# A Fourier mixing layer in fp32 on one core: the shared tile of the second layer as two matmuls of 64 rows, its bias written by VectorE

## The chip, the core and the metric

The kernel runs on one core of a Trainium2 chip. The metric is the device time of one execution in microseconds (us). Before the change it is 5919.63 us, the median of 3 runs (5910.64 to 5933.79).

## The reference

`x` has 4 images of 128 x 128 pixels and 768 channels. The channels are 8 blocks of 96, each with its own complex weights. What is computed, in fp32:

```
xf = rfft2(x, axes=(1, 2), norm='ortho')      # 128 x 65 frequencies
o1r = relu(xr @ w1[0] - xi @ w1[1] + b1[0]);  o1i = relu(xi @ w1[0] + xr @ w1[1] + b1[1])
o2r = o1r @ w2[0] - o1i @ w2[1] + b2[0];      o2i = o1i @ w2[0] + o1r @ w2[1] + b2[1]
o = softshrink(o2, 0.01)
out = irfft2(o, s=(128, 128), norm='ortho') + x
```

## The kernel before

One unit of work is one image and one block of 96 channels: 32 units, run in a loop of 16 pairs. A unit stays in on-chip memory from its load to its store. Its stages on TensorE are:

- A: the transform over the width, 128 matmuls of fp32 (L499). ScalarE copies the results to `U`.
- B, C, D: the rest of the forward transform and the two layers, in 33 steps of two frequencies each (step 32 has one frequency). B (L512, L513) is the first layer's product. C (L523) is the transform over the height. D (L538 to L544) is the second layer's product.
- flip (L549, L550): two matmuls that mend the two frequencies of step 0. ScalarE copies the result.
- E, F: the inverse transforms (L558, and L570 to L572), and VectorE adds the result to `x`.

The order is written out by hand on each engine, with semaphores between them. In the loop over s, TensorE issues B of step s, C of step s-1 and D of step s-2. ScalarE in the same turn copies B's result (L349), gathers the columns for step s+2 (L316), applies ReLU to C's result (L355, L358) and computes the first half of the soft shrinkage of D's result (`excess`, L367). VectorE computes ReLU once more and the low part (L440, L443), and then the shrinkage (L452).

The two frequencies of a step have 2 x 192 hidden values, real and imaginary part of 96 each. They lie in three tiles of 128 rows: the outer tiles 0 and 2 hold 128 values of one frequency each, and the shared middle tile 1 holds 64 values of either. In D an outer tile is multiplied in fp32 with 192 columns of its frequency's weights. The shared tile must add its upper 64 rows to one frequency's 192 columns and its lower 64 rows to the other's. Before, its activations and the weights are each split into a high and a low part of type fp32r (`hidden_high`, `hidden_low`, `w2_high`, `w2_low`, the weights padded with zeros), and three matmuls of 384 columns multiply them; a fourth, with `picks` and `b2_parts`, adds the bias of the second layer. On TensorE an fp32 matmul is two instructions, each with a weight load of its own; an fp32r matmul is one.

The banks of the accumulation memory (PSUM) in this stage: B 0 and 1, C's outer tiles 2 and 3, C's shared tile 6 and 7, D 4 and 5, each by the parity of the step. flip uses bank 6, E banks 4 to 6.

Of the kernel before, what the change touches and what calls it, by code (L numbers as in the profile page):

```python
# [88 lines left out]
def fourier_mlp(nc, x, w1, b1, w2, b2, dft, out):  # L89
    with ExitStack() as ctx:  # L90
# [18 lines left out]
        hidden = [sb(f"hidden{i}", [SIZE, 2, SIZE]) for i in range(2)]  # L109
        hidden_high, hidden_low = ([sb(f"hidden_{x}{i}", [SIZE, SIZE], F32R) for i in range(2)] for x in ("high", "low"))  # L110
        relu1 = [sb(f"relu1_{i}", [SIZE, SIZE]) for i in range(2)]

# [11 lines left out]

        w2_high, w2_low = (sb(f"w2_{x}", [SIZE, 4 * BLOCK], F32R) for x in ("high", "low"))
        over = sb("over", [SIZE, 1])
# [7 lines left out]
        b2_parts = sb("b2_parts", [SIZE, 2 * BLOCK], F32R)  # L134
        picks = sb("picks", [SIZE, SIZE], F32R)
        psum = ctx.enter_context(nc.psum_tensor("psum", [SIZE, 8, 512], F32))

        def bank(i, p=SIZE, n=512):
            return psum[0:p, i, 0:n]
# [15 lines left out]
        def bank_c(s):  # L155

            outer = bank(2 + s % 2, SIZE, 2 * SIZE)
            return [outer[:, 0:SIZE], bank(6 + s % 2, SIZE, SIZE), outer[:, SIZE:]]

        def bank_d(s):  # L160
            return bank(4 + s % 2, SIZE, 4 * BLOCK)

        def parts_d(s, rows):

            return bank_d(s).rearrange("p (q c) -> p c q", c=BLOCK)[:, :, 0:rows]

# [14 lines left out]
        w_loaded = [sem(f"w_loaded{i}") for i in range(2)]  # L181
        W_LOADS = 1 + 3 * len(SEGMENTS) + 2
# [3 lines left out]
        w_negated, w2_split = sem("w_negated"), sem("w2_split")  # L186
        high_done, relu1_done, low_done = sem("high_done"), sem("relu1_done"), sem("low_done")
        u_zeroed = sem("u_zeroed")
# [4 lines left out]
        d_done, excess_done, shrunk = sem("d_done"), sem("excess_done"), sem("shrunk")  # L193
        b2_split = sem("b2_split")
        flip_done, flip_copied = sem("flip_done"), sem("flip_copied")
# [27 lines left out]
        def _(sp):  # L223
# [83 lines left out]
        def _(act):  # L307
# [12 lines left out]
            with act.Fori(0, PAIRS) as m:  # L320
                for par in range(2):
# [22 lines left out]
                    for s in range(NS + 2):  # L344
# [34 lines left out]
        def _(dve):  # L379
            for t in (w2_high, w2_low):  # L380
                dve.memset(t[HALF:SIZE, 0:2 * BLOCK].bitcast(F32), 0.0).then_inc(padding_set, 1)
                dve.memset(t[0:HALF, 2 * BLOCK:].bitcast(F32), 0.0).then_inc(padding_set, 1)
# [3 lines left out]
            dve.wait_ge(padding_set, 7)  # L386
            for row in (0, LOW_ROW):
# [20 lines left out]
            with dve.Fori(0, PAIRS) as m:  # L408
                for par in range(2):
# [11 lines left out]

                    dve.wait_ge(w_negated, (n + 1) * (1 + len(NEGATED)))
                    halves = [(slice(0, HALF), slice(0, 2 * BLOCK)), (slice(HALF, SIZE), slice(2 * BLOCK, 4 * BLOCK))]
                    for rows, cols in halves:
                        dve.tensor_copy(w2_high[rows, cols], w2t[par][rows, 2 * BLOCK:4 * BLOCK]).then_inc(w2_split, 1)
                    dve.tensor_copy(b2_parts[0:1, :], b2t[par][0:1, :]).then_inc(b2_split, 1)
# [3 lines left out]
                                      ALU.subtract).then_inc(b2_split, 1)  # L430
                    dve.wait_ge(w2_split, n * 4 + 2)
                    for rows, cols in halves:
                        dve.tensor_tensor(w2_low[rows, cols], w2t[par][rows, 2 * BLOCK:4 * BLOCK], w2_high[rows, cols],
                                          ALU.subtract).then_inc(w2_split, 1)
                    for s in range(NS + 1):
                        if s < NS:

                            dve.wait_ge(high_done, n * NS + (s + 1))
                            dve.tensor_scalar(relu1[s % 2][:, :], bank_c(s)[1], b1t[par][:, 1:2], 0.0,  # L440
                                              ALU.add, ALU.max).then_inc(relu1_done, 1)
                            dve.wait_ge(relu1_done, n * NS + (s + 1))
                            dve.tensor_tensor(hidden_low[s % 2][:, :], relu1[s % 2][:, :], hidden_high[s % 2][:, :],  # L443
                                              ALU.subtract).then_inc(low_done, 1)
                        if s > 0:
# [37 lines left out]
        def _(pe):  # L483
# [43 lines left out]
            def stage_d(par, n, s):  # L527
                if s == 0:
                    pe.wait_ge(w2_split, n * 4 + 4)
                    pe.wait_ge(b2_split, n * 3 + 3)  # L530
                pe.wait_ge(relu_done, n * NS + (s + 1))
                pe.wait_ge(low_done, n * NS + (s + 1))
                if s >= 2:
                    pe.wait_ge(shrunk, n * NS + (s - 1))
                one, both = 2 * BLOCK, len(STEPS[s]) * 2 * BLOCK
                h, high, low, w, sums_d = hidden[s % 2], hidden_high[s % 2], hidden_low[s % 2], w2t[par], bank_d(s)
                bias = b2_parts[:, :].unsqueeze(1).broadcast_to([SIZE, len(STEPS[s]), 2 * BLOCK])
# [37 lines left out]
            pe.wait_ge(mats_loaded, 16)  # L575
            pe.wait_ge(padding_set, 9)
            with pe.Fori(0, PAIRS) as m:
# [37 lines left out]
```

## Time and profile before

| | |
|---|---|
| median of 3 runs | 5919.63 us |
| profiled execution, its own time | 5931.3 us |
| its span | 5929.5 us |
| granted TensorE clock, mean | 0.986 of full speed |
| TensorE matmuls busy | 97% of the span |
| ScalarE, VectorE, GpSimd busy | 62%, 52%, 21% |

The span is the time of the profiled program from its first to its last instruction. "Busy" of an engine is the time in which at least one of its instructions is under way. PE is TensorE, PEld its weight loads, ACT ScalarE, DVE VectorE, POOL GpSimd. A matmul's recorded duration holds the time until its result is out, and matmuls overlap, so the pace is read from the distance between starts.

### The profile page before, as it was taken

What the parts mean: (1) busy time and instruction counts of PE and PEld (TensorE: products, weight loads), DVE (VectorE), ACT (ScalarE), POOL (GpSimd) and SP (SyncE); (2) the same over time, 40 slices, a digit from 0 to 9 for tenths busy, and PEclk for the clock granted to TensorE, in tenths of its full rate; (3) what the DMA queues carried; (4) which work ended last, traced back from release to release, by engine and by line L of the source; (5) the groups of instructions that cost most, each with busy time, mean ns of one, the idle gap of its engine ahead of it and who ended that gap; (6) DMA issues with size and microseconds to landing.
All of it is one profiled execution on the core that took longest, in us unless ns stands there. A gap on an engine that the chain in (4) does not pass through costs nothing.

```text
span 5929.5 us, 116828 instructions
## 1 busy us (share of the span) xinstructions
PE 5750.8 (97%) x42048; PEld 5699.5 (96%) x42048; DVE 3077.5 (52%) x6166; ACT 3655.1 (62%) x8208; POOL 1263.1 (21%) x810
## 2 busy tenths in 40 slices
PE   8999999999999999999999999999999999999997
PEld 8999999999999999999999999999999999999997
DVE  4555545555455554555545555455554455544555
ACT  6656666566665666656566565665656656566564
POOL 2211222202222022220222202222022221122200
PEclk9999999999999999999999999999999999999999
DMA  3331133321333113332133321333312333123311
GB/s 94 89 89 40 50 89 89 89 50 41 89 89 89 46 44 89 89 89 59 33 88 89 89 68 31 80 89 89 79 34 66 89 89 87 39 53 89 89 44 43
DMA packets 1109645, 423.36 MB, mean 71 GB/s; under 512 B 1108768, under 2 KB 1108896, under 8 KB 1109024
## 3 DMA queue, kind: packets, MB, share of 16 engines
q1 hardware_dynamic: 1109024, 415.14, 27.8%
q8 instruction: 382, 6.26, 0.4%
q14 instruction: 239, 1.96, 0.1%
HBM read 213.75 MB, written 201.33 MB: 70 GB/s over the span
## 4 chain that ended last, share of the span: by engine, by line
PE 96%; issue 2%; ACT 1%; DVE 1%; DMA 0%; DVEq 0%; SPq 0%; ACTq 0%
PE psum L499 16%; PE psum L523 12%; PE psum L512 12%; PE psum L558 12%; PE psum L513 12%; PE psum L542 6%; PE psum L544 6%; PE psum L538 3%; PE psum L570 3%; PE psum L541 3%; PE psum L540 3%; PE psum L539 3%; PE psum L571 3%; PE psum L572 3%; DVE x L465 1%
## 5 line engine op out<-in xcount | busy, mean ns | idle before, releaser
L440 DVE TENSOR_SCALAR relu<-psum,b1t 128x128 f32<-128x128 f32 x1056 | 370.3, 351 | 1936.2 <-ACT hidden_high L355 1936.1
L289 POOL TENSOR_TENSOR doubled<-x 128x768 f32<-128x768 f32 x248 | 359.0, 1447 | 4337.2 <-DMA x<-x 4317.0
L512 PE MATMUL psum<-w1t,columns 96*128 96x192 f32 x4160 | 1035.8, 331 | 66.7 <-ACT columns L313 66.7
L513 PE MATMUL psum<-w1t,columns 96*128 96x192 f32 x4160 | 1029.7, 329 | 0.0
L499 PEld LDWEIGHTS psum<-mats,x 128*96 128x96 f32 x8192 | 930.0, 168 | 76.4 <-issue 54.2
L499 PE MATMUL psum<-mats,x 128*96 128x128 f32 x8192 | 939.1, 278 | 65.5 <-issue 48.8
L349 ACT ACTIVATE mixed<-psum 128x384 f32<-128x384 f32 (+1 forms) x1056 | 513.6, 486 | 746.7 <-PE psum L513 741.6
L376 ACT ACTIVATE sums_high<-psum 128x512 fp32r<-128x512 f32 x768 | 460.0, 599 | 763.7 <-PE psum L558 763.7
L523 PE MATMUL psum<-mats,mixed 128*128 128x128 f32 x6272 | 877.3, 276 | 0.0
L523 PEld LDWEIGHTS psum<-mats,mixed 128*128 128x128 f32 x6272 | 845.5, 193 | 0.0
L512 PEld LDWEIGHTS psum<-w1t,columns 96*128 96x128 f32 x4160 | 756.1, 199 | 73.5 <-ACT columns L313 73.5
L452 DVE SCALAR_TENSOR_TENSOR spectrum<-psum,excess 128x384 f32<-128x384 f32 (+1 forms) x1024 | 562.7, 549 | 491.3 <-ACT excess L367 489.4
L558 PE MATMUL psum<-mats,spectrum 128*128 128x128 f32 x6144 | 799.7, 275 | 11.4 <-ACT spectrum L370 11.4
L367 ACT ACTIVATE excess<-psum,over 128x384 f32<-128x384 f32 (+1 forms) x1056 | 608.8, 576 | 262.4 <-PE psum L544 245.7
L558 PEld LDWEIGHTS psum<-mats,spectrum 128*128 128x128 f32 x6144 | 742.7, 191 | 21.3 <-issue 21.3
L513 PEld LDWEIGHTS psum<-w1t,columns 96*128 96x128 f32 x4160 | 755.0, 198 | 0.0
L458 DVE TENSOR_TENSOR sums_low<-psum,sums_high 128x512 fp32r<-128x512 f32 x768 | 531.3, 692 | 307.5 <-ACT sums_high L376 307.5
L316 ACT ACTIVATE columns<-spectrum 96x512 f32<-96x512 f32 (+1 forms) x1024 | 686.5, 670 | 0.0
L358 ACT ACTIVATE hidden<-psum,b1t 128x128 f32<-128x128 f32 x2080 | 640.1, 361 | 0.0
L443 DVE TENSOR_TENSOR hidden_low<-relu,hidden_high 128x128 fp32r<-128x128 f32 x1056 | 566.0, 536 | 36.3
L465 DVE SCALAR_TENSOR_TENSOR x<-x,psum 128x260 f32<-128x260 f32 (+1 forms) x1536 | 564.6, 413 | 0.0
L542 PE MATMUL psum<-w2t,hidden 128*128 128x192 f32 x2112 | 515.5, 326 | 0.0
(61 smaller groups left out, 8437.8 us busy)
## 6 DMA issues: line engine op xcount, KB each, us to landing
x<-x SPq DMA_DIRECT2D x160, 768.0 KB, 7.2
out<-x SPq DMA_DIRECT2D x160, 768.0 KB, 8.2
x<-x SPq DMA_DIRECT2D x32, 1488.0 KB, 9.7
out<-x SPq DMA_DIRECT2D x32, 1488.0 KB, 10.6
x<-x SPq DMA_DIRECT2D x32, 816.0 KB, 5.0
out<-x SPq DMA_DIRECT2D x32, 816.0 KB, 4.5
w2t<-L_conv_w SPq DMA_DIRECT2D x128, 36.0 KB
w2t<-L_conv_w SPq DMA_DIRECT2D x128, 24.0 KB
```

What stands on the lines that cost most here:

```text
L316: last = act.activation(dst[:, 0:k], U[0:BLOCK, :, j:j + 2 * k].rearrange("p s (k r) -> p k s r", r=2), ACT.Copy)
L358: last = act.activation(hidden[t % 2][:, tile // 2], bank_c(t)[tile], ACT.Relu, bias=b1t[par][:, tile:tile + 1])
L367: act.activation(excess[t % 2][:, :, 0:rows], parts_d(t, rows), ACT.Relu, bias=over[:, 0:1]).then_inc(excess_done, 1)
L443: dve.tensor_tensor(hidden_low[s % 2][:, :], relu1[s % 2][:, :], hidden_high[s % 2][:, :], ALU.subtract).then_inc(low_done, 1)
L452: dve.scalar_tensor_tensor(dst, parts_d(t, rows), LAMBDA, excess[t % 2][:, :, 0:rows], op0=ALU.add, op1=ALU.min).then_inc(shrunk, 1)
L465: dve.scalar_tensor_tensor(part, part, 0.5, bank_f(q - LAG, j), op0=ALU.mult, op1=ALU.add).then_inc(f_added, 1)
L499: last = pe.matmul(bank_a(at)[:, i * SIZE:(i + 1) * SIZE], xs[par][:, slot, :], mat(FW_EVEN if slot <= HALF else FW_ODD), start=True, stop ...
L512: pe.matmul(bank_b(s)[:, k], re, w1t[par][:, BLOCK:], start=True, stop=False)
L513: last = pe.matmul(bank_b(s)[:, k], im, w1t[par][:, :2 * BLOCK], start=False, stop=True)
L523: last = pe.matmul(bank_c(s)[tile], flat[:, tile * SIZE:(tile + 1) * SIZE], mat(FH), start=True, stop=True)
L542: last = pe.matmul(sums_d[:, 0:one], h[:, 0], w[:, 0:one], start=False, stop=both == one)
L558: last = pe.matmul(bank_e(q)[:, :, i], U[:, q * CHUNK + i, 2:], mat(IH), start=True, stop=True)
```

## The change

The shared tile's activations are kept once, in fp32 (`middle`, by VectorE). D multiplies rows 0 to 63 of it with rows 0 to 63 of the weights for the first frequency, and rows 64 to 127 for the second, as fp32 matmuls that use 64 rows of the array each. Each frequency has a PSUM bank of its own, so D takes two banks for each parity of the step (4 and 5, 6 and 7), and C has banks 2 and 3 for all steps. From step 2 on, no matmul adds the bias: VectorE writes it into D's banks (`seeded`) two steps ahead, and all of D's matmuls add to it. In steps 0 and 1 the bias matmul stays, once for each frequency. C of a step now waits for the readers of the step before instead of the one before that, and flip waits for the shrinkage of step 31, since bank 6 is D's now.

```diff
-            return [outer[:, 0:SIZE], bank(6 + s % 2, SIZE, SIZE), outer[:, SIZE:]]
+            outer = bank(2, SIZE, 2 * SIZE)
+            return [outer[:, 0:SIZE], bank(3, SIZE, SIZE), outer[:, SIZE:]]
         def bank_d(s):
-            return bank(4 + s % 2, SIZE, 4 * BLOCK)
+            pair = psum[:, 4 + 2 * (s % 2):6 + 2 * (s % 2), :].rearrange("p k n -> p (k n)")
+            return pair.rearrange("p (q n) -> p q n", q=4)[:, :, 0:BLOCK]
@@ SyncE, load_w @@
+                put(b2_rows[par][:, :, :], b2[:, blk].partition_broadcast(SIZE))
@@ ScalarE, each step @@
-                            act.activation(hidden_high[t % 2][:, :], bank_c(t)[1], ACT.Relu,
-                                           bias=b1t[par][:, 1:2]).then_inc(high_done, 1)
@@ VectorE, once a unit @@
-                        dve.tensor_copy(w2_high[rows, cols], w2t[par][rows, 2 * BLOCK:4 * BLOCK]).then_inc(w2_split, 1)
-                        dve.tensor_tensor(w2_low[rows, cols], w2t[par][rows, 2 * BLOCK:4 * BLOCK], w2_high[rows, cols],
-                                          ALU.subtract).then_inc(w2_split, 1)
@@ VectorE, each step @@
-                            dve.wait_ge(high_done, n * NS + (s + 1))
-                            dve.tensor_scalar(relu1[s % 2][:, :], bank_c(s)[1], b1t[par][:, 1:2], 0.0,
-                                              ALU.add, ALU.max).then_inc(relu1_done, 1)
-                            dve.wait_ge(relu1_done, n * NS + (s + 1))
-                            dve.tensor_tensor(hidden_low[s % 2][:, :], relu1[s % 2][:, :], hidden_high[s % 2][:, :],
-                                              ALU.subtract).then_inc(low_done, 1)
+                            dve.wait_ge(c_done, n * NS + (s + 1))
+                            dve.tensor_scalar(middle[s % 2][:, :], bank_c(s)[1], b1t[par][:, 1:2], 0.0,
+                                              ALU.add, ALU.max).then_inc(middle_done, 1)
 ...
+                            if s + 1 < NS:
+                                k = len(STEPS[s + 1])
+                                dve.wait_ge(shrunk, n * NS + s)
+                                dve.tensor_copy(bank_d(s + 1).rearrange("p (k r) c -> p k r c", r=2)[:, 0:k],
+                                                b2_rows[par][:, :, :].unsqueeze(1).broadcast_to([SIZE, k, 2, BLOCK])).then_inc(seeded, 1)
@@ TensorE, stage_c @@
-                if s >= 2:
-                    pe.wait_ge(relu_done, n * NS + (s - 1))
-                    pe.wait_ge(relu1_done, n * NS + (s - 1))
+                if s >= 1:
+                    pe.wait_ge(relu_done, n * NS + s)
+                    pe.wait_ge(middle_done, n * NS + s)
@@ TensorE, stage_d @@
-                pe.matmul(sums_d[:, 0:both].rearrange("p (k o) -> p k o", o=2 * BLOCK), picks[:, :], bias, start=True, stop=False)
-                pe.matmul(sums_d[:, 0:both], high[:, :], w2_high[:, 0:both], start=False, stop=False)
-                pe.matmul(sums_d[:, 0:both], low[:, :], w2_high[:, 0:both], start=False, stop=False)
-                pe.matmul(sums_d[:, 0:both], high[:, :], w2_low[:, 0:both], start=False, stop=False)
-                last = pe.matmul(sums_d[:, 0:one], h[:, 0], w[:, 0:one], start=False, stop=both == one)
-                if both > one:
-                    last = pe.matmul(sums_d[:, one:both], h[:, 1], w[:, 2 * one:], start=False, stop=True)
+                for k in kws if s < 2 else ():
+                    pe.matmul(sums_d[k], picks[:, :], b2_parts[:, :].rearrange("p (r c) -> p r c", r=2), start=True, stop=False)
+                for k in kws:
+                    pe.matmul(sums_d[k], h[:, k], outer[k].rearrange("p (r c) -> p r c", r=2), start=False, stop=False, skip_group_check=s >= 2)
+                for k in kws:
+                    half = slice(k * HALF, (k + 1) * HALF)
+                    last = pe.matmul(sums_d[k], mid[half, :], w[half, 2 * BLOCK:4 * BLOCK].rearrange("p (r c) -> p r c", r=2),
+                                     start=False, stop=True, skip_group_check=s >= 2)
@@ TensorE, flip @@
-                pe.wait_ge(shrunk, n * NS + 1)
+                pe.wait_ge(shrunk, n * NS + (NS - 1))
```

TensorE's queue in a step of the middle of a unit, before: C of one step, D of the step before it, then the wait ahead of the next B. Names are those of the tiles; each fp32 row is two instructions on the chip.

```order
L523 MATMUL psum<-mats,mixed 128x128 [waits relu1_done,relu_done,b_copied]
L523 MATMUL psum<-mats,mixed 128x128 x2
L538 MATMUL psum<-b_parts,picks 128x384 [waits shrunk,low_done,relu_done]
L539 MATMUL psum<-w_high,hidden_high 128x384
L540 MATMUL psum<-w_high,hidden_low 128x384
L541 MATMUL psum<-w_low,hidden_high 128x384
L542 MATMUL psum<-w2t,hidden 128x192
L544 MATMUL psum<-w2t,hidden 128x192
L509 REGISTER_ALU [waits b_copied]
```

The same place now:

```order
L517 MATMUL psum<-mats,mixed 128x128 [waits middle_done,relu_done,b_copied]
L517 MATMUL psum<-mats,mixed 128x128 x2
L527 REGISTER_ALU [waits middle_done,relu_done]
L534 MATMUL psum<-w2t,hidden 128x2x96 [waits seeded]
L534 MATMUL psum<-w2t,hidden 128x2x96
L538 MATMUL psum<-w2t,middle 128x2x96 x2
L503 REGISTER_ALU [waits b_copied]
```

The four fp32r matmuls ahead of the outer tiles are gone, and the two matmuls of 64 rows stand behind them, last ahead of the next B. D's waits for `low_done` and `shrunk` are now waits for `middle_done` and `seeded`.

VectorE's queue in two steps of the middle of a unit, before:

```order
L439 REGISTER_ALU
L440 TENSOR_SCALAR relu_0<-psum,b1t 128x128 [waits high_done]
L443 TENSOR_TENSOR hidden_low<-relu_0,hidden_high 128x128 [waits relu1_done]
L452 SCALAR_TENSOR_TENSOR spectrum<-psum,excess 128x96x4 [waits excess_done]
L439 REGISTER_ALU
L440 TENSOR_SCALAR relu_1<-psum,b1t 128x128 [waits high_done]
```

And now:

```order
L431 REGISTER_ALU
L432 TENSOR_SCALAR middle<-psum,b1t 128x128 [waits c_done]
L441 SCALAR_TENSOR_TENSOR spectrum<-psum,excess 128x96x4 [waits excess_done]
L446 COPY psum<-b_rows 128x4x96 [waits shrunk]
L431 REGISTER_ALU
L432 TENSOR_SCALAR middle<-psum,b1t 128x128 [waits c_done]
```

The subtraction ahead of the shrinkage is gone, and a copy into PSUM stands behind it, ahead of the next `middle`.

## Rows read from the trace of the kernel before

**Rows 1.** The page's parts 1 and 2: busy time, and the granted clock.

```profile
PE 5750.8 (97%) x42048; PEld 5699.5 (96%) x42048; DVE 3077.5 (52%) x6166; ACT 3655.1 (62%) x8208; POOL 1263.1 (21%) x810
...
PEclk9999999999999999999999999999999999999999
```

**Rows 2.** The chain that ended last, by engine.

```profile
PE 96%; issue 2%; ACT 1%; DVE 1%; DMA 0%; DVEq 0%; SPq 0%; ACTq 0%
```

**Rows 3.** Busy time in one step: stretch, its length, each engine, clock, DMA.

```profile
2499.80:2503.13 3.33, 3.33 (x25) 3.33 (x24) 1.20 (x3) 2.41 (x6) 0.00 (x0) 1.00 0.02 5
```

**Rows 4.** Timeline of TensorE in that step: start, duration, instruction.

```profile
2500.49 0.33 PE L539 MATMUL psum<-w_high,hidden_high 128*128 128x384 f32 x1
...
2500.66 0.34 PE L540 MATMUL psum<-w_high,hidden_low 128*128 128x384 f32 x1
...
2500.83 0.35 PE L541 MATMUL psum<-w_low,hidden_high 128*128 128x384 f32 x1
...
2501.02 0.49 PE L542 MATMUL psum<-w2t,hidden 128*128 128x192 f32 x2
...
2501.34 0.49 PE L544 MATMUL psum<-w2t,hidden 128*128 128x192 f32 x2
...
2501.67 0.49 PE L512 MATMUL psum<-w1t,columns 96*128 96x192 f32 x2
2501.84 0.35 PEld L513 LDWEIGHTS psum<-w1t,columns 96*128 96x128 f32 x2
...
2501.99 0.49 PE L513 MATMUL psum<-w1t,columns 96*128 96x192 f32 x2
...
2502.64 0.49 PE L513 MATMUL psum<-w1t,columns 96*128 96x192 f32 x2
...
2502.97 0.83 PE L523 MATMUL psum<-mats,mixed 128*128 128x128 f32 x6
```

**Rows 5.** Groups by line: ScalarE and VectorE in the steps; busy, mean ns.

```profile
L316 ACT ACTIVATE columns<-spectrum 96x512 f32<-96x512 f32 x992 | 672.7, 678 | 0.0
...
L358 ACT ACTIVATE hidden<-psum,b1t 128x128 f32<-128x128 f32 x2080 | 640.1, 361 | 0.0
...
L367 ACT ACTIVATE excess<-psum,over 128x384 f32<-128x384 f32 x1024 | 595.0, 581 | 245.7 <-PE psum L544 245.7
...
L452 DVE SCALAR_TENSOR_TENSOR spectrum<-psum,excess 128x384 f32<-128x384 f32 x992 | 551.2, 556 | 478.7 <-ACT excess L367 476.8
...
L349 ACT ACTIVATE mixed<-psum 128x384 f32<-128x384 f32 x1024 | 503.0, 491 | 744.5 <-PE psum L513 741.6
...
L440 DVE TENSOR_SCALAR relu<-psum,b1t 128x128 f32<-128x128 f32 x1056 | 370.3, 351 | 1936.2 <-ACT hidden_high L355 1936.1
```

**Rows 6.** Timeline around D of steps 31 and 32 and flip, all engines.

```profile
2542.41 0.49 PE L544 MATMUL psum<-w2t,hidden 128*128 128x192 f32 x2
...
2542.60 0.29 DVE L443 TENSOR_TENSOR hidden_low<-relu,hidden_high 128x128 fp32r<-128x128 f32 x1
...
2542.93 0.58 ACT L367 ACTIVATE excess<-psum,over 128x384 f32<-128x384 f32 x1 [0.70 <-PE psum L544]
...
2542.96 0.19 PEld L538 LDWEIGHTS psum<-b_parts,picks 128*128 128x128 f32 x1 [0.36 <-issue]
...
2543.07 0.19 PEld L539 LDWEIGHTS psum<-w_high,hidden_high 128*128 128x128 f32 x1
...
2543.27 0.27 PE L540 MATMUL psum<-w_high,hidden_low 128*128 128x192 f32 x1
...
2543.38 0.27 PE L541 MATMUL psum<-w_low,hidden_high 128*128 128x192 f32 x1
...
2543.55 0.56 DVE L452 SCALAR_TENSOR_TENSOR spectrum<-psum,excess 128x384 f32<-128x384 f32 x1 [0.66 <-ACT excess L367]
...
2543.84 0.84 PE L549 MATMUL psum<-real_kw,mats 128*128 128x192 f32 x2
```

More of the change, by code:

```diff
@@ L109, in fourier_mlp @@
         hidden = [sb(f"hidden{i}", [SIZE, 2, SIZE]) for i in range(2)]
-        hidden_high, hidden_low = ([sb(f"hidden_{x}{i}", [SIZE, SIZE], F32R) for i in range(2)] for x in ("high", "low"))
-        relu1 = [sb(f"relu1_{i}", [SIZE, SIZE]) for i in range(2)]
+        middle = [sb(f"middle{i}", [SIZE, SIZE]) for i in range(2)]
         excess = [sb(f"excess{i}", [SIZE, BLOCK, 4]) for i in range(2)]
@@ L123, in fourier_mlp @@
         w2t = [sb(f"w2t{i}", [SIZE, 6 * BLOCK]) for i in range(2)]
-        w2_high, w2_low = (sb(f"w2_{x}", [SIZE, 4 * BLOCK], F32R) for x in ("high", "low"))
         over = sb("over", [SIZE, 1])
@@ L135, in fourier_mlp @@
         picks = sb("picks", [SIZE, SIZE], F32R)
+        b2_rows = [sb(f"b2_rows{i}", [SIZE, 2, BLOCK]) for i in range(2)]
         psum = ctx.enter_context(nc.psum_tensor("psum", [SIZE, 8, 512], F32))
@@ L155, in bank_c @@
         def bank_c(s):
-            outer = bank(2 + s % 2, SIZE, 2 * SIZE)
-            return [outer[:, 0:SIZE], bank(6 + s % 2, SIZE, SIZE), outer[:, SIZE:]]
+            outer = bank(2, SIZE, 2 * SIZE)
+            return [outer[:, 0:SIZE], bank(3, SIZE, SIZE), outer[:, SIZE:]]
         def bank_d(s):
-            return bank(4 + s % 2, SIZE, 4 * BLOCK)
+            pair = psum[:, 4 + 2 * (s % 2):6 + 2 * (s % 2), :].rearrange("p k n -> p (k n)")
+            return pair.rearrange("p (q n) -> p q n", q=4)[:, :, 0:BLOCK]
         def parts_d(s, rows):
-            return bank_d(s).rearrange("p (q c) -> p c q", c=BLOCK)[:, :, 0:rows]
+            return bank_d(s).rearrange("p q c -> p c q")[:, :, 0:rows]
         bank_flip = bank(6, SIZE, 2 * BLOCK).rearrange("p (k c) -> p k c", k=2)
@@ L181, in fourier_mlp @@
         w_loaded = [sem(f"w_loaded{i}") for i in range(2)]
-        W_LOADS = 1 + 3 * len(SEGMENTS) + 2
+        W_LOADS = 1 + 3 * len(SEGMENTS) + 3
         mats_loaded, iw_loaded = sem("mats_loaded"), sem("iw_loaded")
@@ L185, in fourier_mlp @@
         padding_set = sem("padding_set")
-        w_negated, w2_split = sem("w_negated"), sem("w2_split")
-        high_done, relu1_done, low_done = sem("high_done"), sem("relu1_done"), sem("low_done")
+        w_negated = sem("w_negated")
+        middle_done = sem("middle_done")
         u_zeroed = sem("u_zeroed")
@@ L193, in fourier_mlp @@
         d_done, excess_done, shrunk = sem("d_done"), sem("excess_done"), sem("shrunk")
-        b2_split = sem("b2_split")
+        b2_split, seeded = sem("b2_split"), sem("seeded")
         flip_done, flip_copied = sem("flip_done"), sem("flip_copied")
@@ L379, in _ @@
         def _(dve):
-            for t in (w2_high, w2_low):
-                dve.memset(t[HALF:SIZE, 0:2 * BLOCK].bitcast(F32), 0.0).then_inc(padding_set, 1)
-                dve.memset(t[0:HALF, 2 * BLOCK:].bitcast(F32), 0.0).then_inc(padding_set, 1)
             dve.memset(over[:, :], -LAMBDA).then_inc(padding_set, 1)
@@ L385, in _ @@
             dve.memset(picks[:, :].bitcast(F32), 0.0).then_inc(padding_set, 1)
-            dve.wait_ge(padding_set, 7)
+            dve.wait_ge(padding_set, 3)
             for row in (0, LOW_ROW):
@@ L420, in _ @@
                         dve.tensor_scalar(part, part, -1.0, None, ALU.mult).then_inc(w_negated, 1)
-                    dve.wait_ge(w_negated, (n + 1) * (1 + len(NEGATED)))
-                    halves = [(slice(0, HALF), slice(0, 2 * BLOCK)), (slice(HALF, SIZE), slice(2 * BLOCK, 4 * BLOCK))]
-                    for rows, cols in halves:
-                        dve.tensor_copy(w2_high[rows, cols], w2t[par][rows, 2 * BLOCK:4 * BLOCK]).then_inc(w2_split, 1)
                     dve.tensor_copy(b2_parts[0:1, :], b2t[par][0:1, :]).then_inc(b2_split, 1)
@@ L430, in _ @@
                                       ALU.subtract).then_inc(b2_split, 1)
-                    dve.wait_ge(w2_split, n * 4 + 2)
-                    for rows, cols in halves:
-                        dve.tensor_tensor(w2_low[rows, cols], w2t[par][rows, 2 * BLOCK:4 * BLOCK], w2_high[rows, cols],
-                                          ALU.subtract).then_inc(w2_split, 1)
                     for s in range(NS + 1):
                         if s < NS:
-                            dve.wait_ge(high_done, n * NS + (s + 1))
-                            dve.tensor_scalar(relu1[s % 2][:, :], bank_c(s)[1], b1t[par][:, 1:2], 0.0,
-                                              ALU.add, ALU.max).then_inc(relu1_done, 1)
-                            dve.wait_ge(relu1_done, n * NS + (s + 1))
-                            dve.tensor_tensor(hidden_low[s % 2][:, :], relu1[s % 2][:, :], hidden_high[s % 2][:, :],
-                                              ALU.subtract).then_inc(low_done, 1)
+                            dve.wait_ge(c_done, n * NS + (s + 1))
+                            dve.tensor_scalar(middle[s % 2][:, :], bank_c(s)[1], b1t[par][:, 1:2], 0.0,
+                                              ALU.add, ALU.max).then_inc(middle_done, 1)
                         if s > 0:
@@ L528, in stage_d @@
                 if s == 0:
-                    pe.wait_ge(w2_split, n * 4 + 4)
                     pe.wait_ge(b2_split, n * 3 + 3)
                 pe.wait_ge(relu_done, n * NS + (s + 1))
-                pe.wait_ge(low_done, n * NS + (s + 1))
+                pe.wait_ge(middle_done, n * NS + (s + 1))
                 if s >= 2:
-                    pe.wait_ge(shrunk, n * NS + (s - 1))
-                one, both = 2 * BLOCK, len(STEPS[s]) * 2 * BLOCK
-                h, high, low, w, sums_d = hidden[s % 2], hidden_high[s % 2], hidden_low[s % 2], w2t[par], bank_d(s)
@@ L542, in stage_d @@
-                last = pe.matmul(sums_d[:, 0:one], h[:, 0], w[:, 0:one], start=False, stop=both == one)
-                if both > one:
-                    last = pe.matmul(sums_d[:, one:both], h[:, 1], w[:, 2 * one:], start=False, stop=True)
+                    pe.wait_ge(seeded, n * (NS - 2) + (s - 1))
+                h, mid, w, kws = hidden[s % 2], middle[s % 2], w2t[par], range(len(STEPS[s]))
+                sums_d = [bank_d(s)[:, 2 * k:2 * k + 2] for k in kws]
+                outer = [w[:, 0:2 * BLOCK], w[:, 4 * BLOCK:]]
@@ L575, in _ @@
             pe.wait_ge(mats_loaded, 16)
-            pe.wait_ge(padding_set, 9)
+            pe.wait_ge(padding_set, 5)
             with pe.Fori(0, PAIRS) as m:
```

1 line of the change is left out of this document (removed).

## The prediction, made before the changed kernel ran

> **What bounds the kernel now.** I read the page's busy line first, then the chain of waits, then one step in detail. TensorE's matmuls are busy 97% of the span at a granted clock of 0.9 or more of full speed in every slice [rows 1], the upper of the two levels (2.4 GHz), and the chain that ended last runs over TensorE for 96% [rows 2]. No other engine is above 62%. So a change counts by what it adds to or takes from TensorE's queue, and by the waits that reach it.
>
> The stage that changes is a repeated step of 3.33 us, in which TensorE is busy 3.33 us, ScalarE 2.41 us and VectorE 1.20 us [rows 3]. A unit has 33 steps, the kernel 1056. Before that, 30 steps of each unit (2 to 31) are alike: 960 in all; steps 0 and 1 (64) and step 32 (32) are counted apart.
>
> In a step the pace is the distance between starts [rows 4]. An fp32 product of 192 columns (two instructions) takes 2501.34 - 2501.02 = 0.32 to 0.33 us, so 0.1625 us for each instruction; Recorded durations are longer: a pair shows 0.49 us where it holds the queue for 0.325, so a result is out 0.165 us behind the queue's time. C's six instructions show 0.83, less 0.165 that is 0.67, or 0.11 each. An fp32r matmul of 384 columns comes each 0.17 us. The weight load of the next instruction begins when the present matmul begins (load at 2501.84, its matmul at 2501.99), and is hidden.
>
> **What goes from a step.** The four fp32r matmuls. The step is 3.33; B is four products and D's outer tiles two, six times 0.325 = 1.95; C is 6 x 0.11 = 0.67. What is left is 3.33 - 1.95 - 0.67 = 0.71 us, which is 4 x 0.17 and 0.03 us for going from fp32 to fp32r and back. This 0.71 us stands wholly on the path.
>
> **What comes to a step: two fp32 products of 64 rows and 192 columns.** That is four instructions, and no row of before shows a matmul of 64 rows; B's 96 rows run at the pace of 128 (0.325 for a product, rows 4), so fewer rows alone save nothing. What can save is that the lower and the upper half of the array work at once. Bounds:
> - No overlap: 4 x 0.1625 = 0.65 us.
> - Full overlap: 2 x 0.1625 = 0.325 us.
 Weight loads come at 0.11 us at the closest [rows 6]: there two loads start at 2542.96 and 2543.07, and the fp32r matmuls of 192 columns, whose columns would take half of 0.17, start 0.11 apart, at 2543.27 and 2543.38. With the loads in order, the third instruction starts at 2 x 0.11 = 0.22, the fourth at 0.22 + 0.1625 = 0.38, and the pair is through at 0.54 us.
> I take 0.54 us: it is the value between the bounds that the order of the queue and the spacing of the loads give.
>
> The TensorE page of the Trainium skill (TensorE: Matmul & The Clock Gate, Part 3, packing small matmuls) says that matmuls on different row groups start about 4 ns apart, in program order. No row here shows it. By that alone the third instruction would start with the second, at 0.16, and the pair would take 0.49.
>
> **Switching the array between 128 and 64 rows, twice a step.** The trace of before has no such switch. The lower bound is nothing. The upper is a full stop: the array empties (the 0.165 us by which a result is late) and the next weights are loaded in the open (0.11 us, the load spacing behind the idle time in rows 6), 0.275 us a switch, 0.55 a step. The nearest row is the switch from fp32 to fp32r and back, 0.03 us for both; I take twice that, 0.06 us a step.
>
> Here a page speaks against the change. The Trainium skill (TensorEngine Tiling (Array Packing), Key Properties) says that changing the tiling mode, not just the tile, drains TensorE, without a price. By the cheap switch of the rows the step gets shorter, by a full drain longer; this is the third rival below.
>
> So a middle step changes by -0.71 + 0.54 + 0.06 = -0.11 us, times 960 = -106 us.
>
> **Steps 0 and 1** keep a bias matmul, one for each frequency: two of 192 columns at 0.11 and the type switch 0.03, +0.25. Together -0.71 + 0.25 + 0.60 = +0.14 us, times 64 = +9 us.
>
> **Step 32 and flip.** Before, flip starts at 2543.84; D of step 31 left the queue at 2542.41 + 0.325 = 2542.74, so 1.10 us earlier [rows 6]. Now flip waits for the shrinkage of step 31: `excess` starts 0.19 us behind the queue's end (2542.93), takes 0.58, and the shrinkage starts 0.04 later (2543.55) and takes 0.56; with 0.03 for the semaphore 0.19 + 0.58 + 0.04 + 0.56 + 0.03 = 1.40, say 1.43. D of step 32, 0.65 us of matmuls, hides in that, with the wait for `middle`, for which VectorE must first seed step 32. Before, TensorE waited here too (0.36 us without a load, for `hidden_low`). So +0.33 us a unit, times 32 = +10 us. Behind flip are ScalarE's copy and E, as before.
>
> **What costs nothing, and its cover.** ScalarE loses one ReLU of the step and has 0.49 + 0.68 + 2 x 0.36 + 0.58 = 2.47 us of work [rows 5] in a step of about 3.2. VectorE has 0.35 (middle) + 0.56 (shrinkage) and the seed. The seed is a copy of 384 elements from on-chip memory into PSUM, which no row shows; bounds 0.35 (the row of 128 elements) and 0.56 (the row of 384 elements); I take 0.5. That is 1.4 us of 3.2. The seed stands ahead of `middle` in the queue: D out at 0.17, `excess` to about 0.8, shrinkage to 1.4, seed to 1.9, and C's result comes at 1.30 + 0.67 + 0.17 = 2.1 us, so `middle` isn't late. The new wait of C is for ReLU of the step before. ScalarE does it behind the copy of B (1.5 to 2.0) and the gather (to 2.7), so to 3.4 us; the next C is due at 3.2 + 1.3 = 4.5 us, 1.1 us later. B's gather, behind C's wait in no queue of another engine, keeps its place. The seed of a step is needed a whole step later. The added load of the bias rows (128 partitions) is issued a unit ahead. All of this is cover that stays if the step falls to about 2.9 us; at full overlap (2.95 us) it is still just there.
>
> **The sum.** -106 + 9 + 10 = -87 us against the profiled execution's own 5931.3, so 5844; that execution lies 0.2% above the median of the runs, so 5832 us against 5919.63 (-1.5%).
>
> **The rivals.**
> 1. Full overlap of the two halves. It needs the hardware to run both pairs side by side though they stand behind one another. The 128 rows of the array speak for it, the order of the queue against it. Step -0.71 + 0.325 + 0.06 = -0.325, times 960 = -312, steps 0 and 1 at -0.075 = -5, flip +10: -307 us, 5613 us.
> 2. The change doesn't do what it says: the halves run one behind the other. Step -0.71 + 0.65 + 0.06 = 0; steps 0 and 1 at +0.25 = +16, flip +10: +26 us, 5946 us, just about no change. For it: both pairs are fp32 pairs with loads of their own, and 96 rows show no gain. Against: different banks and different rows leave nothing shared but the queue.
> 3. Slower: the array stops at each switch of its rows, in D ahead of the 64-row matmuls and again ahead of the next B. With the load alone in the open, 2 x 0.11 = 0.22: step +0.05 = +48, steps 0 and 1 at +0.30 = +19, flip +10: +77, 5997 us. With a full stop, 0.55: step +0.38 = +365, steps 0 and 1 at +0.63 = +40, +10: +415, 6335 us. It decides from 0.17 us of switching a step, 0.085 a switch, less than one load in the open; with halves that don't overlap, from 0.06. For it: between different uses of the array each load must be timed anew, and no slack is left on an engine that is busy without a gap. Against: the switch of type costs 0.03.
> 4. VectorE or ScalarE becomes the bound: 2.47 and 1.4 us in 3.2 speak against it, and I leave it inside the range.
>
> **How the numbers follow.** Forecast 0.40 (its own range 5760 to 5900), full overlap 0.08, no overlap 0.15, stops at the switch 0.37, about evenly spread between its two prices. A measurement of this kernel tells a change from none at about 0.5%, 30 us. Faster: 0.38 of the forecast and 0.08 = 0.46. The same: 0.02 and 0.10 of "no overlap" = 0.12. Slower: 0.05 and 0.37 = 0.42. The range leaves out about a tenth on either side: 5640 to 6300.
>
> **What the profile would show.** Distance between the starts of C in the middle of a unit: 3.22 us for the forecast, 3.0 for full overlap, 3.33 for none, 3.38 to 3.71 for stops. The start of the second 64-row product behind the first: 0.22 for the forecast, 0.325 for no overlap, next to nothing for full. A stop shows as a start of B, or of the first 64-row matmul, more than 0.2 us behind the one before it, with its load later than that one's start. VectorE's copy into PSUM between 0.35 and 0.56 us. Flip 1.4 us behind the queue's end of D of step 31. The forecast is wrong if a switch costs over 0.08 us, or if C or D wait for ScalarE or VectorE in the middle steps.

## The result, and the profile after

| | before | after |
|---|---|---|
| median | 5919.63 us (5910.64 to 5933.79, 5 runs) | 5960.43 us (5954.12 to 5967.26, 5 runs) |
| ratio | | 1.0066, 95% interval 1.0049 to 1.0083 |
| span of the profiled execution | 5929.5 us | 5958.6 us |
| granted TensorE clock in it, mean | 0.986 | 0.990 |
| one step in the middle of a unit | 3.33 us | 3.35 us |

The kernel is slower by 0.7%. The forecast was 1.5% faster. Two terms of the sum failed, in opposite directions: the two halves overlap wholly (0.215 us a step better than forecast), and each change between 128 and 64 rows of the array costs 0.20 us (0.34 us a step worse).

The page's busy line of the changed kernel, the answer to [rows 1]:

```profile
PE 5777.4 (97%) x42112; PEld 5259.3 (88%) x42112; DVE 3033.5 (51%) x5970; ACT 3379.7 (57%) x7152; POOL 1251.2 (21%) x810
...
PEclk9999999999999999999999999999999999999999
```

TensorE is still the bound. In the middle of a unit it had its full clock in both kernels (1.00); over the whole execution the mean rose from 0.986 to 0.990, which is taken up below. What is new stands in PEld: the weight loads were busy as long as the matmuls (96%) and are now at 88%. Loads that wait are the mark of the change. Where they wait is in the list of waits (line waited on, releaser: total us, times, longest):

```profile
PEld psum L538 <- issue: 237.6, 1056, 0.2
PEld psum L506 <- issue: 215.9, 960, 0.2
...
PEld psum L534 <- DVE psum L446: 18.3, 32, 0.7
...
PE psum L534 <- DVE middle L432: 9.0, 32, 0.4
...
PEld psum L544 <- DVE spectrum L441: 7.2, 32, 0.2
```

In every one of 1056 steps the load of the first 64-row matmul (L538) finds its queue idle for 0.23 us, with nothing of another engine that releases it, and in 960 steps so does the load of the next B (L506). Before, no such row stands in the middle steps of a unit. The same in the timeline of one step (start, duration, instruction), which answers to [rows 4]:

```profile
2501.50 0.83 PE L517 MATMUL psum<-mats,mixed 128*128 128x128 f32 x6
...
2502.17 0.82 PE L534 MATMUL psum<-w2t,hidden 128*128 128x192 f32 x4
...
2502.91 0.30 PEld L538 LDWEIGHTS psum<-w2t,middle 64*128 64x128 f32 x4 [0.23 <-issue]
2502.92 0.60 PE L538 MATMUL psum<-w2t,middle 64*128 64x192 f32 x4
2503.44 0.31 PEld L506 LDWEIGHTS psum<-w1t,columns 96*128 96x128 f32 x2 [0.23 <-issue]
2503.44 0.60 PE L506 MATMUL psum<-w1t,columns 96*128 96x192 f32 x2
...
2503.88 0.49 PE L507 MATMUL psum<-w1t,columns 96*128 96x192 f32 x2
```

Read it as a sum of distances. The outer tiles start at 2502.17 and hold the queue for 4 x 0.1625 = 0.65, to 2502.82. The load of the 64-row matmul starts only at 2502.91, 0.09 later, together with its matmul; in [rows 4] a load starts a whole matmul ahead. The four 64-row instructions then take 2503.44 - 2502.92 = 0.52 us. B's first product takes 2503.88 - 2503.44 = 0.44 where it took 0.325 before, 0.11 of it the load in the open. If the same 0.09 and 0.11 stand around the 64-row matmuls, 0.52 - 0.20 = 0.32 us is left for all four: that is the price of two, so the halves run side by side. In all 0.325 + 2 x 0.20 = 0.73 us, against the 0.71 us of the four fp32r matmuls. A narrower window, up to 2502.99, shows two starts at 2502.92, so two instructions begin together:

```profile
2502.92 0.43 PE L538 MATMUL psum<-w2t,middle 64*128 64x192 f32 x2
```

Here x2 covers 0.43 us; a single one of them lasts up to 0.427 (0.11 more than the 0.32 of one whose load is hidden). The other two begin together as well, at 2503.18 and 2503.19. A row doesn't say which half an instruction belongs to, and ends of matmuls are modelled, so this reading needed experiments.

Where the 29.1 us of span went, added up over the 32 units from the starts in the traces: from the first to the last start in C 3321.3 before and 3355.5 us after, +34; from there to flip 82.3 and 88.7, +6; from a unit's first start in B to its first in C 111.9 and 94.9, -17; everything else +6. The -17 is TensorE's clock and not a saving of the change. That stretch takes 5.28 us at the lower of the two levels and 2.71 at the upper, here in two units of the kernel before (stretch, its length, each engine, clock, DMA):

```profile
2621.67:2626.95 5.28, 5.28 (x16) 5.28 (x17) 0.00 (x0) 1.58 (x3) 2.82 (x2) 0.50 1.17 325
3172.06:3174.77 2.71, 2.71 (x16) 2.71 (x17) 0.00 (x0) 1.58 (x3) 0.00 (x0) 1.00 0.26 60
```

Before, 15 of the 32 units take longer than 2.71 us there; after, 6. Over the whole execution TensorE stood at the lower level for 41 us less than before, apart from the end, where it is idle. That is worth about 20 us (an estimate: at half the clock half of the time is lost), so at an equal clock the changed kernel would be nearer 50 us slower than 29. The runs show the same bond of time and clock: on one chip the kernel before took 5950 to 5952 us at a granted clock of 0.983 and 5912 to 5915 at 0.989; the one run of the changed kernel at 0.989 took 5967. TensorE's wait ahead of the stretch is the same in both (66.7 us in 32 waits for `columns`); why the changed kernel falls to the lower level less often, no run here shows.

### The profile page after: what moved, and what is told of

Its sections match the earlier page's. It is cut to its first block, busy times and chain, and to the rows that moved or that the text cites. A ratio compares the mean times of both kernels' runs of the same rounds, so it can differ in the third digit from the quotient of the medians.

```text
span 5958.6 us, 116726 instructions
## 1 busy us (share of the span) xinstructions
PE 5777.4 (97%) x42112; PEld 5259.3 (88%) x42112; DVE 3033.5 (51%) x5970; ACT 3379.7 (57%) x7152; POOL 1251.2 (21%) x810
## 4 chain that ended last, share of the span: by engine, by line
PE 95%; issue 2%; ACT 1%; DVE 1%; DMA 0%; DVEq 0%; SPq 0%; ACTq 0%
PE psum L493 15%; PE psum L506 15%; PE psum L553 12%; PE psum L517 12%; PE psum L507 11%; PE psum L534 11%; PE psum L538 9%; PE psum L565 3%; PE psum L566 3%; PE psum L567 3%; DVE x L459 1%; PE psum L544 0%; ACT columns L319 0%; PE psum L545 0%; ACT excess L371 0%
## 5 line engine op out<-in xcount | busy, mean ns | idle before, releaser
L506 PE MATMUL psum<-w1t,columns 96*128 96x192 f32 x4160 | 1132.4, 354 | 66.7 <-ACT columns L319 66.7
L507 PE MATMUL psum<-w1t,columns 96*128 96x192 f32 x4160 | 1021.2, 327 | 0.0
L493 PE MATMUL psum<-mats,x 128*96 128x128 f32 x8192 | 933.5, 277 | 64.3 <-issue 47.3
L506 PEld LDWEIGHTS psum<-w1t,columns 96*128 96x128 f32 x4160 | 701.3, 196 | 289.4 <-issue 215.9
L432 DVE TENSOR_SCALAR middle<-psum,b1t 128x128 f32<-128x128 f32 x1056 | 370.0, 350 | 1015.7 <-PE psum L517 1015.7
L534 PE MATMUL psum<-w2t,hidden 128*128 128x192 f32 x4160 | 855.6, 328 | 9.0 <-DVE middle L432 9.0
L507 PEld LDWEIGHTS psum<-w1t,columns 96*128 96x128 f32 x4160 | 750.4, 197 | 0.0
L534 PEld LDWEIGHTS psum<-w2t,hidden 128*128 128x128 f32 x4160 | 652.9, 191 | 18.3 <-DVE psum L446 18.3
L538 PE MATMUL psum<-w2t,middle 64*128 64x192 f32 x4160 | 629.0, 375 | 0.0
```

What stands on the lines that cost most here:

```text
L493: last = pe.matmul(bank_a(at)[:, i * SIZE:(i + 1) * SIZE], xs[par][:, slot, :], mat(FW_EVEN if slot <= HALF else FW_ODD), start=True, stop ...
L506: pe.matmul(bank_b(s)[:, k], re, w1t[par][:, BLOCK:], start=True, stop=False)
L507: last = pe.matmul(bank_b(s)[:, k], im, w1t[par][:, :2 * BLOCK], start=False, stop=True)
L534: pe.matmul(sums_d[k], h[:, k], outer[k].rearrange("p (r c) -> p r c", r=2), start=False, stop=False, skip_group_check=s >= 2)
L538: last = pe.matmul(sums_d[k], mid[half, :], w[half, 2 * BLOCK:4 * BLOCK].rearrange("p (r c) -> p r c", r=2), start=False, stop=True, skip_ ...
```

## The experiments

Two theories. "Stops": the halves overlap wholly and a change of rows costs 0.20 us. "No overlap": the halves follow one another (0.65 us) and changes are nearly free (0.04 each). Both give the measured 0.73 us a step. Each ratio below is to the kernel before on the same chip; its median there was 5942 us for e1 to e4 and 5930 us for e5 to e8.

| | step, us | median, us | ratio, 95% interval |
|---|---|---|---|
| e1, both halves on rows 0 to 63 | 3.67 | 6285 | 1.0577 (1.0552 to 1.0602) |
| e2, 128 rows with zeros | 3.27 | 5894 | 0.9930 (0.9909 to 0.9951) |
| e3, seeds alone | 3.15 | 5820 | 0.9796 (0.9776 to 0.9816) |
| e4, halves of two steps together | 3.15 (mean) | 5845 | 0.9852 (0.9828 to 0.9875) |
| e5, halves apart | 4.06 | 6696 | 1.1286 (1.1256 to 1.1315) |
| e6, another end of the steps | 3.35 | 5954 | 1.0042 (1.0024 to 1.0059) |
| e7, e4 with that end | 3.15 (mean) | 5798 | 0.9763 (0.9740 to 0.9786) |
| e8, e3 with that end | 3.15 | 5784 | 0.9750 (0.9728 to 0.9772) |

### e1: both halves on the same rows

```diff
-                    half = slice(k * HALF, (k + 1) * HALF)
+                    half = slice(0, HALF)
```

> The changed kernel, but both 64-row matmuls of a step use rows 0 to 63 of the array (so the second frequency gets the first half of the shared tile's values: that part of the output is another one). Theory: in the changed kernel the two halves run wholly side by side (0.325 us for both), and each change between 128 and 64 rows costs 0.20 us (0.09 to empty the array, 0.11 for a weight load in the open), so 0.73 us in all. On one half of the array they must follow one another: +0.325 us in each of 1024 steps, 3.68 us a step, about 6293 us. Rival: the halves follow one another already (0.65) and a change of rows costs 0.04; then nothing changes here, 3.35 us a step, 5960 us.

Two lines of its timeline, and one of a window up to 2440.20:

```profile
2440.14 0.92 PE L538 MATMUL psum<-w2t,middle 64*128 64x192 f32 x4
2440.98 0.60 PE L506 MATMUL psum<-w1t,columns 96*128 96x192 f32 x2
...
2440.14 0.43 PE L538 MATMUL psum<-w2t,middle 64*128 64x192 f32 x1
```

The same four instructions now take 0.84 us instead of 0.52, and the step 3.67 instead of 3.35. Only one instruction starts at 2440.14; on the same rows none starts beside another. So in the changed kernel each of the two pairs has one instruction of either half, and they overlap wholly: 0.32 us is the whole price of one product. "No overlap" falls.

### e2: 128 rows, no change of rows

```diff
-                    last = pe.matmul(sums_d[k], mid[half, :], w[half, 2 * BLOCK:4 * BLOCK].rearrange(...),
+                    last = pe.matmul(sums_d[k], mid[:, :], w2_pad[:, 2 * k * BLOCK:2 * (k + 1) * BLOCK].rearrange(...),
```

`w2_pad` is fp32, filled by VectorE once a unit (two copies), its other half zero.

> The changed kernel, with each 64-row matmul made one of 128 rows, its weights padded with zeros (the same result). No change of rows is left, and no overlap. Theory: 0.65 us instead of 0.325 + 2 x 0.20 = 0.73, so -0.08 us in 1024 steps, 3.27 us a step, about 5880 us. The rival (no overlap, cheap changes of rows) expects the same 3.27 us, from 0.65 instead of 0.65 + 0.08; so this run prices the sum, and e1 and e4 tell the theories apart. If both were wrong and a change of rows cost a full 0.275, it would be 3.27 us too, but with more gained.

```profile
2442.25 0.82 PE L541 MATMUL psum<-w2t,hidden 128*128 128x192 f32 x4
2442.90 0.81 PE L544 MATMUL psum<-w_pad,middle 128*128 128x192 f32 x4
2443.55 0.49 PE L512 MATMUL psum<-w1t,columns 96*128 96x192 f32 x2
```

Twice the work in the array, with nothing side by side, and it is faster than the changed kernel: 0.65 us from 2442.90 to 2443.55, no idle load, a step of 3.27 us. It also beats the kernel before, by 0.7%; from the first to the last start in C it takes 3275.8 us over the units, where that took 3321.3.

### e3: the seeds without the 64-row matmuls

The kernel before, with VectorE's copy of the bias into D's bank behind each shrinkage and D's wait for it, and:

```diff
-                pe.matmul(sums_d[:, 0:both].rearrange("p (k o) -> p k o", o=2 * BLOCK), picks[:, :], bias, start=True, stop=False)
+                if s < 2:
+                    pe.matmul(sums_d[:, 0:both].rearrange("p (k o) -> p k o", o=2 * BLOCK), picks[:, :], bias, start=True, stop=False)
```

> The kernel before with only the second half of the change: from step 2 on VectorE writes the bias into D's bank and the fourth fp32r matmul (the bias) is gone; the three fp32r matmuls of the split parts, and all banks, stay. Both theories: -0.17 us in 960 steps = -163 us, and +0.3 us a unit at the end of the steps, where the seed of step 32 stands ahead of the work that D waits for (+10): about 5766 us, 3.16 us a step. If VectorE became the bound (0.35 + 0.29 to 0.54 + 0.56 + 0.56 = 1.8 to 2.0 us a step), TensorE would show waits for it, and the time would stay over 5800.

Three fp32r matmuls and the outer tiles take 2441.86 - 2440.60 = 1.26 us here:

```profile
2440.60 0.42 PE L547 MATMUL psum<-w_high,hidden_high 128*128 128x384 f32 x1
2440.86 0.34 PE L548 MATMUL psum<-w_high,hidden_low 128*128 128x384 f32 x1
2441.04 0.33 PE L549 MATMUL psum<-w_low,hidden_high 128*128 128x384 f32 x1
2441.21 0.49 PE L550 MATMUL psum<-w2t,hidden 128*128 128x192 f32 x2
...
2441.86 0.49 PE L519 MATMUL psum<-w1t,columns 96*128 96x192 f32 x2
```

The step falls by 0.18 us, as expected. The time falls by 2.0%, where 2.6% was expected. The rest has three parts. At the end of a unit D of step 32 waits behind the seed (26.0 us in all in the list of waits, with 35.3 for its load); from the last start in C to flip that is +14 us in all, where +10 was expected. Where the loop goes on to the next pair of units, A starts later with nothing on another engine that releases it, here before and then in e3:

```profile
PE psum L499 <- issue: 48.8, 15, 3.6
...
PE psum L506 <- issue: 62.4, 15, 4.7
```

e8, the other kernel with seeds alone, has 65.0 us in this row and the changed kernel 47.3, so these 14 us belong to the kernel; their cause is open. And the clock was lower: 0.982 to 0.985 in e3's executions, 0.983 to 0.989 in those of the kernel before on the same chip. So the half of the change that saved time is the seeds.

### e4: the halves of two steps together

```diff
+                for t in done_with(s):            # none, or the two steps t = s - 1 and s
+                    for k in range(len(STEPS[t])):
+                        half = slice(k * HALF, (k + 1) * HALF)
+                        last = pe.matmul(bank_d(t)[:, 2 * k:2 * k + 2], middle[t % 4][half, :], w[half, 2 * BLOCK:4 * BLOCK].rearrange(...),
+                                         start=False, stop=True, skip_group_check=t >= 2)
+                    last.then_inc(d_done, 1)
```

> The changed kernel, with the 64-row matmuls of two steps issued together every second step, so that the rows of the array change twice in two steps instead of four times (same result; the shared tile has four buffers, ScalarE and VectorE take the two steps' results one behind the other). Theory (0.20 us a change of rows): -0.20 us a step, times 1024 = -205 us, 3.15 us a step on the mean; at a unit's end the seed of step 32 comes later, about +1.0 us, times 32 = +32: about 5787 us. Rival (0.04 a change): -0.04 x 1024 + 32, about 5951 us.

```profile
2439.70 0.82 PE L538 MATMUL psum<-w2t,hidden 128*128 128x192 f32 x4
2440.45 0.92 PE L542 MATMUL psum<-w2t,middle 64*128 64x192 f32 x8
2441.30 0.60 PE L510 MATMUL psum<-w1t,columns 96*128 96x192 f32 x2
...
2443.38 0.82 PE L538 MATMUL psum<-w2t,hidden 128*128 128x192 f32 x4
2444.03 0.49 PE L510 MATMUL psum<-w1t,columns 96*128 96x192 f32 x2
...
2446.00 0.82 PE L538 MATMUL psum<-w2t,hidden 128*128 128x192 f32 x4
```

Two steps take 2446.00 - 2439.70 = 6.30 us, 3.15 each, 0.20 less than the changed kernel: one pair of changes saved in two steps is 0.40, as "stops" says. Eight instructions take 0.85 us from 2440.45 to 2441.30, that is 0.65 and 0.20. The time fell by less than expected: by the ratios it is 2.1% under the changed kernel, where 2.9% was expected, 47 us less. The end of a unit was underestimated: from the last start in C to flip it takes 4.16 us where the changed kernel takes 2.77, +1.4 and not +1.0, which is 13 us. The other 34 us or so fit the clock: the granted clock was 0.984 in this profiled execution and 0.990 in that of the changed kernel, and 0.006 of 5842.5 us is 35 (an estimate).

### e5: the halves apart

```diff
-                for k in kws:
-                    pe.matmul(sums_d[k], h[:, k], outer[k]...)
-                for k in kws:
+                for k in kws:
+                    pe.matmul(sums_d[k], h[:, k], outer[k]...)
                     half = slice(k * HALF, (k + 1) * HALF)
```

> The changed kernel, with the order in D outer tile, half, outer tile, half, so that the two 64-row matmuls never stand beside one another (same result). Theory (full overlap, 0.20 us a change of rows): each step has four changes of rows and no overlap, 0.65 + 4 x 0.20 = 1.45 us in place of 0.73, +0.72 us in 1024 steps = +740 us, about 4.07 us a step and 6700 us. Rival (no overlap, 0.04 a change): +0.08 a step, 6040 us.

```profile
2440.46 0.49 PE L534 MATMUL psum<-w2t,hidden 128*128 128x192 f32 x2
2440.88 0.59 PE L536 MATMUL psum<-w2t,middle 64*128 64x192 f32 x2
2441.40 0.59 PE L534 MATMUL psum<-w2t,hidden 128*128 128x192 f32 x2
2441.92 0.59 PE L536 MATMUL psum<-w2t,middle 64*128 64x192 f32 x2
2442.44 0.60 PE L506 MATMUL psum<-w1t,columns 96*128 96x192 f32 x2
```

One half alone takes 2441.40 - 2440.88 = 0.52 us, exactly what both took together in the changed kernel, and an outer product between two changes takes the same 0.52 = 0.325 + 0.20. Both directions cost alike. The median of 6696 us against the expected 6700 closes the sum.

### e6: another end of the steps

```diff
+            if s == NS - 1:
+                return bank(0).rearrange("p (q n) -> p q n", q=2)[:, :, 0:BLOCK]
 ...
-        bank_flip = bank(6, SIZE, 2 * BLOCK).rearrange("p (k c) -> p k c", k=2)
+        bank_flip = bank(1, SIZE, 2 * BLOCK).rearrange("p (k c) -> p k c", k=2)
 ...
-                if s >= 2:
-                    pe.wait_ge(seeded, n * (NS - 2) + (s - 1))
+                if 2 <= s < NS - 1:
+                    pe.wait_ge(seeded, n * (NS - 3) + (s - 1))
 ...
-                for k in kws if s < 2 else ():
+                for k in kws if s < 2 or s == NS - 1 else ():
 ...
-                pe.wait_ge(shrunk, n * NS + (NS - 1))
+                pe.wait_ge(shrunk, n * NS + 1)
```

> The changed kernel with another end of the steps: the sums of step 32 go to bank 0 with their bias by a matmul, as in steps 0 and 1, so that it waits for no seed, and flip goes to bank 1 and waits only for the shrinkage of step 0, as before the change. From the last start in C to flip the changed kernel takes 2.77 us (before 2.57). Without waits 0.11 + 1.18 for D of step 31, 0.20 + 0.11 + 0.33 + 0.20 + 0.33 for step 32 and 0.09 = 2.54: -0.23 us, times 32 = -7 us. If flip's own wait had been the cost, as the prediction had it, it would be -0.33 x 32 = -10 us; either is at the edge of what can be measured, so the trace decides: which wait stands ahead of D of step 32 and of flip.

First the changed kernel there, the answer to [rows 6]:

```profile
2561.09 0.60 PE L538 MATMUL psum<-w2t,middle 64*128 64x192 f32 x4
2561.12 0.36 DVE L446 COPY psum<-b_rows 128x192 f32<-128x192 f32 x1
2561.39 0.34 DVE L432 TENSOR_SCALAR middle<-psum,b1t 128x128 f32<-128x128 f32 x1
2561.74 0.58 ACT L371 ACTIVATE excess<-psum,over 128x384 f32<-128x384 f32 x1 [0.82 <-PE psum L538]
2561.96 0.30 PEld L534 LDWEIGHTS psum<-w2t,hidden 128*128 128x128 f32 x2 [0.57 <-DVE psum L446]
2561.97 0.59 PE L534 MATMUL psum<-w2t,hidden 128*128 128x192 f32 x2 [0.28 <-DVE middle L432]
2562.35 0.56 DVE L441 SCALAR_TENSOR_TENSOR spectrum<-psum,excess 128x384 f32<-128x384 f32 x1 [0.62 <-ACT excess L371]
...
2563.01 0.30 PEld L544 LDWEIGHTS psum<-real_kw,mats 128*128 128x128 f32 x2 [0.23 <-DVE spectrum L441]
```

D of step 32 waits for `middle` (2561.39 + 0.34 = 2561.73, with the way through the queue 2561.96), behind the seed. Flip's load stands idle for 0.23 us, with a shrinkage as its releaser, but 0.23 us is what every load shows at a change of rows; the wait is covered. With the other end both waits are gone from the list (the last row here was the one for L544, the load of flip, now put down to "issue"):

```profile
PEld psum L540 <- issue: 237.6, 1056, 0.2
...
PEld psum L546 <- issue: 7.2, 32, 0.2
```

From the last start in C to flip it takes 2.54 us instead of 2.77, as expected to the hundredth. In the median it is at the edge: 1.0042 against 1.0066, with intervals that overlap. Only the trace shows it.

### e7 and e8: the two best with that end

> The kernel with the 64-row matmuls of two steps together, with that other end of the steps. There the way from the last start in C to flip was 4.16 us, since the seed of step 32 comes behind two steps' results. It should be about 2.5 us now: -1.6 x 32 = -52 us, about 5793 us where that kernel had 5845. If it moves less, the wait has moved to the start of E, which needs three shrinkages of a row.

> The kernel before with VectorE's seeds alone, with step 32 in bank 0 and its bias by a matmul. In that kernel D of step 32 waited 0.8 us a unit for the low part, behind the seed, 0.25 to 0.36 in the kernel before: -0.5 x 32 = -16 us, plus 0.1 a unit for the bias matmul: about 5807 us where it had 5820.

e7: 5798 us where 5793 was expected; the way to flip is 2.86 us instead of 4.16. Of the 0.36 us that did not come, 0.325 are no wait: the 64-row matmuls of step 30 stand in this stretch too, beside those of step 31, and 2.5 us leaves them out. The one wait near it, C of step 32 for `middle`, stands ahead of the stretch and is the same in e4 (there L521):

```profile
PE psum L523 <- DVE middle L438: 15.2, 32, 0.5
```

e8: 5784 us, 36 less than e3, where 13 less was expected. In the traces the way from the last start in C to flip takes 83.8 us in all instead of 96.6, just these 13; the rest goes with the chip (5942 and 5930 for the kernel before) and the clock (0.982 to 0.985 in e3's executions, 0.986 to 0.988 in e8's). Its step is that of e3, and it has the lowest time of all: 2.5% under the kernel before, with no matmul of 64 rows. It and e7 can't be told apart (0.9750 and 0.9763, with intervals that overlap).

## Why the prediction was wrong

- What bounds the kernel: right. The step's distances in the new trace add up with the same 0.1625 and 0.11 us for each instruction, and in the middle of a unit the clock kept its level. What the sum had no term for is the clock between the units: it gave the changed kernel about 20 us (an estimate, worked out above).
- What goes (0.71 us a step): right. e3 took one of the four away and saved 0.18.
- The two products of 64 rows: 0.54 forecast, 0.325 measured (e1: +0.32 when they share rows). The step that failed is "both instructions of rows 0 to 63 stand ahead of both of rows 64 to 127. Then only the second of the first pair and the first of the second pair can run together". In the changed kernel the second half starts with the first, in the trace within 0.01 us and not 0.22 later, and the two instructions left start together 0.27 us after them. Whether the instructions stand in the queue in another order than I took, or start out of it, the trace doesn't tell. The Trainium skill (TensorE: Matmul & The Clock Gate, Part 3, packing small matmuls) has matmuls on different row groups start side by side and in program order. This trace agrees with the first; with the second it agrees only if the order of the four is not the one I took, and 0.49 us, my estimate from both, was too much.
- The change of rows: 0.06 us a step forecast, 0.40 measured (2 x 0.20; e2, e4, e5). This is the step that decided: "The nearest row is the switch from fp32 to fp32r and back, 0.03 us for both; I take twice that". The nearest row, a change from fp32 to fp32r, was the wrong likeness: there the next load still starts while the last matmul runs (0.03 us), here it starts 0.09 us after the queue's end and stands in the open for another 0.11. The bounds held (nothing to 0.55). The Trainium skill (TensorEngine Tiling (Array Packing), Key Properties), which says that a change of the tiling mode drains TensorE, stood beside the rival that came true, and the trace agrees with it, at 0.20 us for one.
- The sum of the two: -0.71 + 0.325 + 0.40 = +0.015 us where -0.11 was forecast; 960 such steps are +14 us instead of -106. The starts in the trace are 3.353 and 3.326 us apart at the median, +0.027 or +26 us.
- Steps 0 and 1: the starts in C around them are 3.575 and 3.328 us apart at the median, +0.25, times 64 = +16 us instead of +9. By the same terms it would be -0.71 + 0.25 + 0.73 = +0.27.
- The end: +10 forecast. From the end of D of step 31 in the queue (2561.09 + 0.11 + 0.325 = 2561.52) flip comes 1.49 us later, forecast 1.43, before 1.10. The size was right, the named wait only half: what stands in the way is `middle` behind the seed ahead of D of step 32, and flip's own wait ends under the change of rows.
- The cover of VectorE and ScalarE: right in the middle of a unit. Its copy into PSUM takes 0.56 us (0.5 taken, 0.56 the bound), and no wait for `seeded` or `middle` stands in the list outside step 32.
- The rivals: no single one came true. Full overlap (0.08) and stops (0.37) came true together, and I had worked out each with the other's term at its forecast value. The time landed near that of the second rival, no overlap at cheap changes (5946 us), which e1 shows to be the wrong mechanism.

## What to carry to other kernels

Here an operation that uses the array in another shape (64 rows between 128) pays twice where it stands alone between others: going there and coming back. Count the changes of shape, not the matmuls, and put all of one shape together before judging it; here 0.40 us for two changes ate a real saving of 0.39 us. Where two terms are unknown, work out their combinations as rivals too; compare the granted clock of two runs before a difference of some tens of us is put down to an edit; and price the parts of a change one by one: the seeds alone were worth 2%, and the 64-row matmuls lost more than that.

## What was not expected of the hardware

- Two fp32 products on different halves of the array, 64 rows by 192 columns into different banks, cost 0.325 us together, as much as one, though each is two instructions and the halves stand one behind the other in the program. On the same rows they cost 0.65 (e1, whose outputs are in different banks too). Whether it also needs the different banks, no run here shows.
- A change between 128 and 64 rows costs 0.20 us in either direction at the full clock: 0.09 until the next load starts and 0.11 for the load. It is the same for one half as for two, for four instructions as for eight (e4, e5).
- 96 rows beside 128 rows cost no such change (B and C, [rows 4]).
- Zeros are cheap: two products with half of their rows padded with zeros (0.65 us) beat two of 64 rows with their changes (0.73 us).
